# Fused transformer kernel: the experts' x of the second to fourth batch is loaded in turned layout and normed along columns

## What is computed

```python
xn = _layernorm(x, axis=-1)
x = x + _L0_attn_ref(xn, ...) + _L0_ffn_ref(xn, ...)
xn = _layernorm(x, axis=-1)
x = x + _L1_attn_ref(xn, ...) + _L1_ffn_ref(xn, ...)
```

## Time and profile before

| | |
|---|---|
| Time, median of 3 runs | 714.2 us (712.54 to 715.79) |
| Profiled execution, its own time | 712.47 us |
| Profiled execution, its span | 710.7 us |
| Mean granted TensorE clock | 0.996 of full speed |
| Instructions | 10703 |

### The profile page before, as it was taken

The page is one execution under the profiler, slowest core; times in us unless marked ns, Lnnn a source line. Parts: engine busy times, 40 slices in busy tenths (PEclk is TensorE's granted clock), DMA queues, the critical chain, the costliest instruction groups (busy, mean ns, idle before and its releaser), DMA issues.

```text
span 710.7 us, 10703 instructions
## 1 busy us (share of the span) xinstructions
PE 688.0 (97%) x4090; PEld 585.9 (82%) x4090; DVE 517.6 (73%) x933; ACT 376.0 (53%) x777; POOL 130.9 (18%) x125
## 2 busy tenths in 40 slices
PE   7999999999999999999999999999999999999997
PEld 7778888878777788887888878887777888889886
DVE  7736667886965658556675656757769998998996
ACT  5896676855745425354254442446557355354541
POOL 7145434510000010000200001000032214203220
PEclk9999999999999999999999999999999999999999
DMA  5096353000000000000000000050000000000000
GB/s 192 13 309 213 106 136 98 0 1 1 1 1 0 1 1 1 0 1 1 1 1 0 1 1 1 0 237 2 1 0 1 1 1 30 1 30 1 2 30 30
DMA packets 21282, 25.78 MB, mean 36 GB/s; under 512 B 976, under 2 KB 19408, under 8 KB 20464
## 3 DMA queue, kind: packets, MB, share of 16 engines
q1 hardware_dynamic: 20576, 23.79, 10.2%
q10 hardware_dynamic: 656, 1.31, 0.5%
HBM read 22.94 MB, written 2.16 MB: 35 GB/s over the span
## 4 chain that ended last, share of the span: by engine, by line
PE 70%; DVE 18%; issue 5%; ACT 4%; POOL 2%; DMA 1%; DVEq 0%; POOLq 0%
PE bank L89 21%; PE bank L91 19%; PE bank L90 19%; DVE l_ring_lo L2472 2%; PE bank L490 2%; DVE l_ge L2453 2%; DVE l_h L2468 2%; DVE l_o L2476 1%; DVE l_h L2425 1%; DVE h_raw L1186 1%; POOL m_den L827 1%; PE bank L466 1%; DVE fused_lo L141 1%; DVE l_oT_lo L2482 1%; POOL l_prod L2336 1%
## 5 line engine op out<-in xcount | busy, mean ns | idle before, releaser
L1186 DVE TENSOR_TENSOR h_raw<-h_s,bank 128x512 f32<-128x512 f32 x104 | 71.4, 687 | 113.8 <-ACT h_s L1176 98.8
L1176 ACT ACTIVATE h_s<-bank 128x512 f32<-128x512 f32 x104 | 62.2, 598 | 161.2 <-PE bank L91 161.1
L1191 DVE TENSOR_TENSOR h_ring_lo<-h_raw,h_ring_hi 128x512 fp32r<-128x512 f32 x92 | 69.0, 750 | 0.1
L1180 ACT ACTIVATE h_ring_hi<-h_raw 128x512 fp32r<-128x512 f32 x104 | 64.8, 623 | 2.3 <-DVE h_raw L1186 2.3
L90 PE MATMUL bank<-fused_lo,h_ring_hi 128*128 128x256 f32 x208 | 58.4, 281 | 0.0
L2173 ACT ACTIVATE l_s<-bank 128x512 f32<-128x512 f32 x32 | 19.1, 598 | 64.6 <-PE bank L91 64.6
L89 PE MATMUL bank<-l_xT_hi,l_wgu 128*128 128x512 f32 x128 | 51.3, 401 | 0.1
L89 PE MATMUL bank<-f_yT_hi,mlp_hi 128*128 128x512 f32 x128 | 50.9, 398 | 0.0
L90 PE MATMUL bank<-l_xT_lo,l_wgu 128*128 128x512 f32 x128 | 50.3, 393 | 0.0
L91 PE MATMUL bank<-l_xT_hi,l_lo 128*128 128x512 f32 x128 | 50.3, 393 | 0.0
L91 PE MATMUL bank<-f_yT_hi,fused_lo 128*128 128x512 f32 x128 | 50.0, 391 | 0.0
(11 more groups left out here) (363 smaller groups left out, 2022.8 us busy)
## 6 DMA issues: line engine op xcount, KB each, us to landing
m_W<-m_scratch SPq DMA_DIRECT2D x16, 512.0 KB, 6.2
fused_raw<-in_fused SPq DMA_DIRECT2D x1, 3584.0 KB, 16.0
res<-in_x SPq DMA_DIRECT2D x4, 512.0 KB, 6.1
fused_raw<-in_fused SPq DMA_DIRECT2D x2, 1024.0 KB, 8.3
l_raw<-in_layer SPq DMA_DIRECT2D x1, 2048.0 KB, 10.0
out_x<-res SPq DMA_DIRECT2D x16, 128.0 KB, 1.8
l_raw<-in_layer SPq DMA_DIRECT2D x1, 1280.0 KB, 12.5
fused_raw<-in_fused SPq DMA_DIRECT2D x1, 1152.0 KB, 5.1
```

The lines of the kernel that those rows point to most:

```text
L1176: self.nc.scalar.activation(self.s[u % 2][r, :], gate[r, :], ACT.Silu).then_inc(self.silu.sem, 1)
L1180: self.nc.scalar.activation(self.unit(i, u)[0], self.product(i, u), ACT.Copy).then_inc(self.hi.sem, 1)
L1186: self.nc.vector.tensor_tensor(out=self.product(i, u), in0=self.s[u % 2][r, :], in1=up[r, :], op=ALU.mult).then_inc(self.hidden.sem, 1)
L1191: self.nc.vector.tensor_tensor(out=lo, in0=self.product(i, u), in1=f32(hi), op=ALU.subtract).then_inc(self.lo.sem, 1)
```

## The change

The experts' x of batches 1, 2 and 3 is no longer made by `norm_x` and `turn_x`. A second copy of the raw input comes in a turned layout (features on the partitions), `in_turned_x`, and is loaded into `xw` by one DMA a batch. Since tokens now lie along the columns, mean and root of a token are no longer one number per partition. They are turned once, in `turn_gates`, copied by ScalarE, stored as rows to a DRAM tensor `x_rows`, and for each batch loaded back broadcast to all partitions. VectorE then subtracts the means (`centre_x`, unit 23) and multiplies by the roots (`scale_x`, unit 24), each one instruction over 128x1024. `high_x` and `low_x` read `xw` in place of the banks. Batch 0 stays as it was. `weighted(0, 0)` gets a wait, since the turned rows lie in its bank, and `router_and_ranks` gets the wait on the banks that `turn_x` had.

```diff
@@ mlstm_phase, SyncE
         after.issue(sp, 0)
+        sp.wait_ge(act_tables, ROWS_IN)
+        sp.dma_start(g.x_rows[0].rearrange("b (c s) -> (b c) s", s=P), x_rows[0:B * C, 0, :]).then_inc(stored, 16)
+        for b in range(B):
+            sp.dma_start(g.x_rows[1, b].rearrange("(c s) -> c s", s=P), x_rows[2 * b * C:(2 * b + 1) * C, 1, :]).then_inc(stored, 16)
         for n in range(RING, N):
             spread_rows(n)
@@ turn_gates, TensorE
             pe.wait_ge(dve_rows, DIAG)
+            pe.wait_ge(rooted.sem, rooted.at(2 * B - 1, 1))
+            nc.tensor.transpose(rows_banks[0], g.mean, ident[:, :])
+            nc.tensor.transpose(rows_banks[1], rr[:, :, :, :].rearrange("p b n c -> p (b n c)"), ident[:, :])
@@ weighted, TensorE
             if n:
                 pe.wait_ge(evicted.sem, evicted.at(b, 2 * c))
+            else:
+                pe.wait_ge(act_tables, ROWS_IN)
@@ mlstm_phase, ScalarE
         weights(1)
+        act.wait_ge(tables_t, ENDS_T)
+        nc.scalar.activation(x_rows[0:B * C, 0, :], rows_banks[0], ACT.Copy)
+        nc.scalar.activation(x_rows[:, 1, :], rows_banks[1], ACT.Copy).then_inc(act_tables, 1)
         copy_q(1)
@@ fused_phase, SyncE
+        sp.wait_ge(g.rows_stored, 16 * (B + 2))
+        for i in range(1, B):
+            sp.wait_ge(mask_t.sem, mask_t.at(i - 1, 4))
+            sp.dma_start(xw[:, :, :], g.turned_x_in[:, i]).then_inc(x_loaded.sem, 16)
+            sp.wait_ge(yT_t.sem, yT_t.at(i, KD))
+            sp.dma_start(x_rows[:, :, :], g.x_rows[:, i, :].unsqueeze(0).to_broadcast([P, 2, S])).then_inc(x_loaded.sem, 16)
@@ fused_phase, TensorE
         def turn_x(i):
             pe.wait_ge(xs_ready.sem, xs_ready.at(i, 2))
-            if i:
-                pe.wait_ge(zprod.sem, zprod.at(i - 1, 2))
@@
         def router_and_ranks(i):
             pe.wait_ge(xT_lo.sem, xT_lo.at(i, KD))
+            if i:
+                pe.wait_ge(zprod.sem, zprod.at(i - 1, 2))
@@
-                if u == 2:
+                if u == 2 and i == 0:
                     turn_x(i)
@@ fused_phase, ScalarE
         def high_x(i):
+            if i:
+                act.wait_ge(x_scaled.sem, x_scaled.at(i - 1, 2))
+                act.wait_ge(hid.gate_up.sem, hid.gate_up.at(i - 1, LAST_BASE + 1))
             for k in range(KD):
-                act.wait_ge(xT_t.sem, xT_t.at(i, k + 1))
-                nc.scalar.activation(xT[0][:, k, :], turn_bank[k][:, :], ACT.Copy).then_inc(xT_hi.sem, 1)
+                if i == 0:
+                    act.wait_ge(xT_t.sem, xT_t.at(i, k + 1))
+                nc.scalar.activation(xT[0][:, k, :], xw[:, k, :] if i else turn_bank[k][:, :], ACT.Copy).then_inc(xT_hi.sem, 1)
@@ fused_phase, GpSimd: sum_x
-            pool.wait_ge(xs_ready.sem, xs_ready.at(i, 2))
+            if i:
+                pool.wait_ge(x_scaled.sem, x_scaled.at(i - 1, 2))
+            else:
+                pool.wait_ge(xs_ready.sem, xs_ready.at(i, 2))
@@ fused_phase, VectorE
+        def centre_x(i):
+            dve.wait_ge(x_loaded.sem, x_loaded.at(i - 1, 32))
+            nc.vector.tensor_tensor(out=xw[:, :, :], in0=xw[:, :, :], in1=x_rows[:, 0, :].unsqueeze(1).to_broadcast([P, KD, S]), op=ALU.subtract).then_inc(x_scaled.sem, 1)
+
+        def scale_x(i):
+            dve.wait_ge(x_scaled.sem, x_scaled.at(i - 1, 1))
+            nc.vector.tensor_tensor(out=xw[:, :, :], in0=xw[:, :, :], in1=x_rows[:, 1, :].unsqueeze(1).to_broadcast([P, KD, S]), op=ALU.mult).then_inc(x_scaled.sem, 1)
@@ low_x
-                nc.vector.tensor_tensor(out=xT[1][:, k, :], in0=turn_bank[k][:, :], in1=f32(xT[0][:, k, :]), op=ALU.subtract).then_inc(xT_lo.sem, 1)
+                nc.vector.tensor_tensor(out=xT[1][:, k, :], in0=xw[:, k, :] if i else turn_bank[k][:, :], in1=f32(xT[0][:, k, :]), op=ALU.subtract).then_inc(xT_lo.sem, 1)
@@ the loop over units
                     elif u == 14:
                         scale_y(i + 1)
-                    elif u in (15, 16):
-                        norm_x(i + 1, u - 15)
+                    elif u == U - 3:
+                        centre_x(i + 1)
+                    elif u == U - 2:
+                        scale_x(i + 1)
```

More of the change, by code:

```diff
@@ L156, with program @@
 L1_ALL = L1_QKV + L1_OUT + L1_GATE_UP + L1_DOWN
-def program(nc, x_in, cols_in, bias_in, mlstm_in, fused_in, layer1_in, out):
+def program(nc, x_in, turned_x_in, cols_in, bias_in, mlstm_in, fused_in, layer1_in, out):
     ctx = ExitStack()
@@ L196, in program @@
         for_fused = Fetch(sems, "fused", [[(g.fused_raw[:, a:b], fused_in[:, a:b])] for a, b in zip(cuts, cuts[1:])])
-        g.x_in, g.cols_in, g.bias_in = x_in, cols_in, bias_in
+        g.x_in, g.turned_x_in, g.cols_in, g.bias_in = x_in, turned_x_in, cols_in, bias_in
+        g.x_rows = nc.dram_tensor("x_rows", (2, B, S), fp32, kind="Internal").ap()
         l1 = layer1_weights(nc, g, layer1_in)
@@ L266, in mlstm_phase @@
     hT = [m.pair(f"m_hT{n}", [P, KD, 2 * P]) for n in range(2)]
+    x_rows = Map(nc, m.at)("m_x_rows", [2 * B * C, 2, P])
     gr, diag, qrow = m("m_gr", [3 * R, S]), m("m_diag", [R, C, R]), m("m_qrow", [R, S - P])
@@ L285, in mlstm_phase @@
     scratch = nc.dram_tensor("m_scratch", (R, S), fp32, kind="Internal").ap()
+    stored = g.rows_stored = one("m_stored")
     const_ready, x_loaded, cols_loaded = one("m_const"), [one(f"m_x{n}") for n in range(B)], one("m_cols")
@@ L294, in mlstm_phase @@
     TG_T, ENDS_T, SPREAD_T = range(1, 4)
-    TG_IN, ENDS_IN, EA_M, DEXP, EA_K = range(1, 6)
+    TG_IN, ENDS_IN, EA_M, DEXP, EA_K, ROWS_IN = range(1, 7)
     DEC, GA = range(1, 3)
     IDENT_READY, CONSTANTS = 3, 28
-    eq_ready, stored, loaded = sg("m_eq", 1), one("m_stored"), [one(f"m_W_loaded{n}") for n in range(RING)]
+    eq_ready, loaded = sg("m_eq", 1), [one(f"m_W_loaded{n}") for n in range(RING)]
     k_t, q_t, kv_t, og_t = sg("m_k_t", 1), sg("m_q_t", 1), sg("m_kv_t", 3), sg("m_og_t", 2)
@@ L314, in mlstm_phase @@
     ends_cols = slice(B * C, B * C + C * R)
+    rows_banks = [n_bank[0:B * C, 0:P], n_bank[0:2 * B * C, P:2 * P]]
     side = lambda b, n: bank[(6, 7)[(b + 1 + n) % 2]]
@@ L1357, in fused_phase @@
     over = Map(nc, spread_at)
+    xw, x_rows = Map(nc, spread_at)("f_xw", [P, KD, S]), Map(nc, spread_at + 4 * KD * S)("f_x_rows", [P, 2, S])
     xs, ys = over("f_xs", [P, C, D]), over("f_ys", [P, C, D])
@@ L1364, in fused_phase @@
     TURN, LAST = U - 6, (B - 1, U - 1)
+    LAST_BASE = order.index((FB - 1, 0))
     rows = lambda u: P if order[u][0] == "mlp" else width(order[u][0])
@@ L1373, in fused_phase @@
     zprod, zsum, zhi, zlo, experts_done = sg("f_zprod", 2), sg("f_zsum", 1), sg("f_zhi", 1), sg("f_zlo", 1), sg("f_experts", 1)
+    x_scaled, x_loaded = sg("f_xw", 2), sg("f_xl", 32)
     both, acc_free, late_ready, late_done = sg("f_both", 1), sg("f_accfree", 2), sg("f_late", 1), sg("f_late_done", 2)
@@ L1695, in norm_x @@
         def norm_x(i, half):
-            if i:
-                dve.wait_ge(mask_t.sem, mask_t.at(i - 1, 4))
             for c in (2 * half, 2 * half + 1):
@@ L1807, in late_statistics @@
             w.close("late statistics")
+        dve.wait_ge(g.rows_stored, 16 * (B + 2))
         for i in range(B):
@@ L2630 @@
     cols = _np.stack([m(n).reshape(KD, P).T for n in ("norm1_w", "norm2_w", "mh_w")], axis=1)
-    arrays = {"in_x": m("x").reshape(B * C, P, D).transpose(1, 0, 2), "in_cols": cols,
+    arrays = {"in_x": m("x").reshape(B * C, P, D).transpose(1, 0, 2), "in_turned_x": m("x").transpose(2, 0, 1).reshape(KD, P, B, S).transpose(1, 2, 0, 3), "in_cols": cols,
               "in_bias": _np.concatenate([m("b_ig")] * B + [m("b_fg")] * B).reshape(-1, 1), "in_mlstm": mlstm, "in_fused": flat(mlp, ffn), "in_layer1": layer1}
```

## The result

| | before | after |
| --- | --- | --- |
| Median of the runs | 714.85 us (712.54 to 716.64, 20 runs) | 713.17 us (709.96 to 714.19, 20 runs) |
| Ratio after / before | | 0.9971, 95% interval 0.9961 to 0.9981 |
| Profiled execution, its own time | 712.47 us | 713.19 us |
| Its span | 710.7 us | 711.5 us |
| TensorE, instructions | 4090 | 4068 |

The kernel is faster by 0.29% by this ratio, which is taken over all runs. Of 714.85 us that is 2.07 us, from 1.4 to 2.8; the medians alone are 1.68 apart. It lies within the 0.5% that the prediction calls no change. The profiled execution of after is longer than the one of before, by 0.8 us of span. So the two traces can't be laid on each other by their ends; the gain has to be read place by place, and what hides it has to be found. The three places first.

The account below looks back on a forecast made before the run. TensorE, busy 97% of the span, was taken to bound the kernel. 3.2 us won in the fused phase less 0.4 lost in the opening gave 2.8, from 714.2 to 711.4 us, range 708.6 to 714.7.

Parts of the forecast that it names:

- What bounds the kernel: Fused phase: TensorE bounds, busy 97% of the span; a microsecond less there is a microsecond less if others' work isn't late.
- What is removed: Units 2 and 3: eight transposes in each of batches 1 to 3, 1.17 us a batch by distance of starts, 3.51 us.
- The seam: Between batches: `centre_x` makes `dve_hidden` of unit 24 and the L1191 TensorE waits for late, costing 0.06 us a batch.
- `experts_back`: Behind the gates in unit 3: TensorE comes earlier, `low_z` is ready by only 0.06 us; 0.05 us a batch counted lost.
- The instructions at 1.22, `scale_x` free, the load hidden: Fused phase: new VectorE instructions take 1.22 us, `scale_x` has 0.9 to spare, `x_rows` lands in 5 to 6 of 11.8.
- Fused phase: Batches 1 to 3 together: 3 x (1.17 - 0.06 - 0.05) = 3.2 us won.
- The opening: 0.4 us lost, bounds 0.2 and 1.2: 0.3 for two transposes, 0.1 for ScalarE's later list; stores cost nothing.
- The sum: Whole kernel: 3.2 us won less 0.4 lost is 2.8 us, from the median 714.2 to 711.4 us.
- Nothing arrives: Rival: late `low_z`, a broken stream and `centre_x` at 1.79 us take back the win; 713.3 to 714.2 us, chance 0.2.
- Slower by the broadcast: Rival: VectorE stands at `centre_x` for `x_rows` past 11.8 us; 719.5 us at 14.5; chance of any slower rival 0.1.
- Slower by contention: VectorE and GpSimd contend in SBUF; decides only if `sum_x` moved to the seam; chance of any slower rival 0.1.
- Faster than TensorE's own time says: Rival: waits beside the change shrink too, some 0.5 us a batch; 4.6 us won, 709.6 us, chance 0.27.

Follow-up runs that it names:

- the split moved ahead: Kernel after with `centre_x` and `scale_x` one unit later and, in unit 2, `high_z` ahead of `act_hi`, `low_z` ahead of `dve_lo`: ratio 0.9960, 710.91 us.
- the opening alone: Kernel before with only the opening's two transposes, two copies, five stores and the wait of `weighted(0, 0)`: ratio 1.0005, median 715.89 us.
- the fused phase alone: Kernel before with only the change's fused phase, its two rows loaded from raw x: ratio 0.9956, 711.50 us over 9 runs.

## Why the prediction was nearly right

Forecast were 2.8 us and, as the likeliest case, no change within 0.5%; measured are 2.07 (1.4 to 2.8) by the ratio, 1.68 by the medians and 2.6 by the fastest runs. So the likeliest case came, and the time of 713.17 lies in the range. It lies 1.8 above the 711.4 forecast: 0.65 of that is the start, since the median of before is 714.85 over 20 runs and was 714.2 over 3, and the rest is the smaller gain. That the fastest runs come within 0.2 of the forecast is in part luck, since the two losses in the fused phase were put too low and the one in the opening too high. By its steps:

- **What bounds the kernel.** Right. A microsecond off TensorE in this phase was one, as the run with the transposes put back shows (3.1 measured, give or take 1.4, and 3.3 by the fastest runs; 3.0 by distances).
- **What is removed, 1.17 a batch.** Right, shown by the same run.
- **The seam, 0.06 a batch.** Right in its chain, too small: 0.13, 0.15 and 0.18. The term that failed is the 0.08 by which the next instruction was to start before the end of `centre_x`. It was taken from the earlier trace rows, from a pair in which that holds, but the row after `centre_x` starts 0.02 after its end. The run with the norm one unit later shows that the chain is the one named: with `centre_x` behind that L1207 the loss is gone.
- **`experts_back`, 0.05 a batch.** Right in its place, too small: 0.16. Of this 0.06 is the longer step up to it, near the 0.05 counted. The other 0.10 is the longer step behind it. The prediction had such a broken stream in its rival and not in the sum. The run with the split moved ahead shows that both go together.
- **The instructions at 1.22, `scale_x` free, the load hidden.** Right. The load took 4.9 where 5 to 6 were counted and had 6.9 to spare.
- **Fused phase 3.2.** It is 3.51 less 0.46 at the seams and 3 x 0.16 at `experts_back`, so 2.6 by these terms, and 2.7 by the shift of ScalarE's starts.
- **The opening, 0.4.** 0.22 by the trace, all of it in the two transposes; the 0.1 for ScalarE's list and the stores did not come. Two profiled executions with the opening's part have no stretch of half clock there, and they say the same: at the line that before has at 56.62 the norm one unit later is 0.35 behind and the one with the split 0.29, of which 0.10 and 0.05 were there ahead of the transposes. By the fastest runs the opening alone costs 0.3.
- **The sum.** 2.6 less 0.2 is 2.4, against 2.6 by the fastest runs. The ratio over all runs has 0.5 less, the medians 0.9. This would come from after being at the half clock for longer, or more often, than before: after's runs lie on average 2.7 above its fastest, before's 2.0, those of the opening alone 2.4, those of the fused phase alone 1.4. That speaks for something in the opening's part that makes such stretches more frequent. But of the versions of after with that part the one with the transposes has 2.5, the two with the norm moved 2.4 and 1.9, and the one with `sum_x` moved 2.3, so with 9 to 35 runs of each it isn't shown.
- **Nothing arrives.** Fell: `centre_x` has 1.22 and not 1.79, and the losses at the tight places are 0.29 to 0.34 a batch where this rival had 0.75.
- **Slower by the broadcast.** Didn't come, since the load lands after 4.9. Made real, it is as predicted up to VectorE's stall; its price of one microsecond for each was too low, since the half clock behind the stand added half as much again at two of the three seams.
- **Slower by contention.** Only if `sum_x` moved, it said; with it moved the kernel is slower by 0.39%, as that L1207 in place of another is hit.
- **Faster than TensorE's own time says.** Fell. The terms above leave nothing for a wait beside the change that shrank.

What stays open is why TensorE's clock halves in the opening, in some executions and not in others. Filling the gaps ahead of it didn't take it away. With it stays open whether the change's opening makes these stretches more frequent, and so whether the 0.5 to 0.9 us by which the gain over all runs is smaller than by the fastest ones are a cost of the change or chance.

## What to carry to other kernels

Taking work off the bounding engine gave its distance of starts here, not its duration, and only where its next inputs are early enough: list for each consumer behind the removed work when its input is ready, and let the producers' order follow (here two swaps of order gave back 0.9 of 3.5 us). A long instruction put into another engine's list belongs behind the one for which the bounding engine waits, not before it. Where one kernel's times stand in groups, compare many runs, and read what an edit costs from the steps at its place, not from the span.

## What the runs showed of the hardware

- TensorE at half clock between 28 and 50 us, for 3.4 or 6.8 us, in some executions and not in others; the execution is longer by half of that (1.5 to 1.7 and 3.2 to 3.5 us).
- After a stand of 3.2 us at the seam TensorE made up to nine steps longer than 0.23, most of them 0.43, and lost 1.6 us by them; after two others of 3.3 and 3.2 us it did so once and once not.
- At `experts_back` of after a stream that was broken for 0.06 us lost another 0.10 in its next step, in all three batches.
- A VectorE instruction of 128x512 with both inputs in SBUF took 2.87 in place of 0.68 beside a 128x1024 addition of 2.89 on GpSimd.
- A broadcast of two rows of DRAM to 128 partitions, 512 KB, landed in 4.8 to 5.0 us with its queue empty.
